# Moving the attention's early steps against the feed-forward chunks, in the batches after the first two

## The reference

```python
h = jnp.einsum('bhid,oi,od->bho', x, weighted_sum, weight)      # 'mix': 256 x 4 inputs -> 256 per token

t = layernorm(h)                                                # attention
q, k, v = split(t @ qkv_w.T + qkv_b)                            # 16 heads of 16
q, k = rotate(q), rotate(k)
q, k = q / norm(q), k / norm(k)
h = h + softmax(q @ k.T * HD ** -0.5) @ v @ out_w.T + out_b

t = layernorm(h)                                                # 8 experts, hidden width 1024
p = sigmoid(t @ Wg + bg)
w = p * (p > 0.5)
h = h + sum_e w[:, e] * (relu(t @ W1[e] + b1[e]) @ W2[e] + b2[e])
```

## Time and profile before

| | |
|---|---|
| median of 3 runs | 1918.91 us (1918.88 to 1920.49) |
| the profiled execution's own time | 1918.81 us |
| its span, first to last instruction | 1917.0 us |
| PE busy | 1838.3 us (96%) |
| ACT busy | 1077.8 us (56%) |
| DVE busy | 698.6 us (36%) |
| POOL busy | 628.7 us (33%) |

### The profile page before, as it was taken

The page is one execution under the profiler, slowest core; times in us unless marked ns, Lnnn a source line. Parts: engine busy times, 40 slices in busy tenths (PEclk is TensorE's granted clock), DMA queues, the critical chain, the costliest instruction groups (busy, mean ns, idle before and its releaser), DMA issues.

```text
span 1917.0 us, 31838 instructions
## 1 busy us (share of the span) xinstructions
PE 1838.3 (96%) x12652; PEld 1168.6 (61%) x12652; DVE 698.6 (36%) x1575; ACT 1077.8 (56%) x1658; POOL 628.7 (33%) x537
## 2 busy tenths in 40 slices
PE   5679899999999999999999999999999999999999
PEld 4156545775467754677547764577546775466666
DVE  7867644554023621346103460144401453022001
ACT  3744676546655476545765457644665546654444
POOL 1012323334233342333323242333423334234443
PEclk9789999999999999999999999999999999999999
DMA  4322433415123151223313341232512315213221
GB/s 163 112 108 89 132 126 139 176 56 132 67 90 120 67 132 67 103 96 100 110 45 111 121 111 67 77 127 73 132 67 88 121 67 131 69 67 103 107 98 46
DMA packets 103971, 192.31 MB, mean 100 GB/s; under 512 B 67448, under 2 KB 80656, under 8 KB 87440
## 3 DMA queue, kind: packets, MB, share of 16 engines
q1 hardware_dynamic: 103824, 190.28, 30.7%
HBM read 153.55 MB, written 20.97 MB: 91 GB/s over the span
## 4 chain that ended last, share of the span: by engine, by line
PE 85%; DVE 3%; DMA 2%; ACT 2%; issue 2%; SPq 0%; DVEq 0%; ACTq 0%
PE bank_h L995 32%; PE bank_f L1014 11%; PE bank_f L1017 10%; PE bank_f L1016 10%; PE bank_o L903 6%; PE bank_s L889 4%; PE bank_s L801 3%; PE bank_s L802 3%; PE bank_s L803 3%; DMA kt<-stack 1%; DMA kt<-probs 1%; ACT hh L778 1%; PE bank_m L915 1%; PE bank_s L949 1%; PE bank_m L810 1%
## 5 line engine op out<-in xcount | busy, mean ns | idle before, releaser
L644 POOL TENSOR_TENSOR hl<-h,hh 128x512 f16<-128x512 f32 x512 | 602.9, 1178 | 1202.7 <-ACT hh L778 688.4
L995 PE MATMUL bank_h<-x,w1s 128*128 128x512 f16 x3072 | 750.0, 381 | 5.2 <-ACT hh L778 4.6
L775 ACT ACTIVATE h<-bank_h,b1s 128x512 f32<-128x512 f32 x512 | 351.3, 686 | 479.4 <-PE bank_h L995 479.2
L1014 PE MATMUL bank_f<-w2s,hh 128*128 128x256 f16 x2048 | 560.4, 274 | 2.3 <-DVE acc L1255 2.3
L1017 PE MATMUL bank_f<-w2s,hl 128*128 128x256 f16 x2048 | 558.8, 273 | 0.0
L1016 PE MATMUL bank_f<-w2s,hh 128*128 128x256 f16 x2048 | 558.8, 273 | 0.0
L995 PEld LDWEIGHTS bank_h<-x,w1s 128*128 128x128 f16 x3072 | 287.9, 99 | 331.0 <-issue 43.7
L778 ACT ACTIVATE hh<-bank_h,b1s 128x512 f16<-128x512 f32 x512 | 349.9, 683 | 0.0
L744 ACT ACTIVATE probs<-bank_s 128x1024 f32<-128x1024 f32 x240 | 246.3, 1026 | 161.5 <-PE bank_s L889 160.6
L1014 PEld LDWEIGHTS bank_f<-w2s,hh 128*128 128x128 f16 x2048 | 201.4, 98 | 107.1 <-issue 40.6
L1255 DVE SCALAR_TENSOR_TENSOR acc<-bank_f,gw,acc 128x256 f32<-128x256 f32 x256 | 106.1, 477 | 368.9 <-PE bank_f L1017 368.7
(11 more groups left out here) (187 smaller groups left out, 1451.5 us busy)
## 6 DMA issues: line engine op xcount, KB each, us to landing
w1s<-w_parts SPq DMA_DIRECT2D x56, 1024.0 KB, 4.8
w2s<-w_parts SPq DMA_DIRECT2D x56, 1024.0 KB, 4.8
raw<-in_w_dram SPq DMA_DIRECT2D x16, 1024.0 KB, 6.6
xraw<-in_x_t_dram SPq DMA_DIRECT2D x30, 512.0 KB, 4.8
w_parts<-w1s SPq DMA_DIRECT2D x8, 1024.0 KB, 8.7
w_parts<-w2s SPq DMA_DIRECT2D x8, 1024.0 KB, 10.9
out_dram<-acc SPq DMA_DIRECT2D x16, 256.0 KB, 6.1
w1s<-in_x_t_dram SPq DMA_DIRECT2D x2, 512.0 KB, 8.6
```

The lines of the kernel that those rows point to most:

```text
L644: pool.tensor_tensor(hl[n % HBUFS][:], h32[n % 2][:], hh[n % HBUFS][:], ALU.subtract)\
L775: act.activation(h32[n % 2][:], bank_h[n % 2][:, :], ACT.Relu, bias=b1s[:, e, m:m + 1]).then_inc(h_hi.sem, 1)
L995: last = pe.matmul(bank_h[n % 2][:, :], w[:, wp, k, m * P:(m + 1) * P], x16s[fb % 2][:, xp, k, :], start=(k == 0 and wp + xp == 0), stop=( ...
L1014: pe.matmul(o, high, w[:, 0, m, :], start=(m == 0 and t % 2 == 0), stop=False, skip_group_check=True)
```

## The change

The due times of the steady list (`later` in the code: neither alone nor the first feed-forward) get their own tables. The other two lists come out as they were. In chunks, before and after:

| step | before | after |
|---|---|---|
| `mix` 0 to 3 | 2.1, 3.5, 4.9, 6.3 | 1.6, 2.7, 3.8, 4.9 |
| `ln1_turn` 0 to 3 | 9.0 + 1.5 t | 7.4 + 1.3 t |
| `qk_norm` | 15.7 | 13.2 |
| `stack` 0 to 3 | 18.85, 19.7, 20.5, 21.3 | 15.0, 15.85, 16.65, 17.45 |
| `out_bias` | 24.0 | 20.0 |
| `scores n` | 25.6 + 0.66 n | 20.2 + 0.80 n |

`weigh`, `out_copy`, `out_turn` and the attention's tail are tied to the pace and the first score, so the tail stays within a fraction of a chunk of where it was. In SP's queue `turn_stacks` moves ahead of expert 3's load.

```diff
-    mix, sooner, att_at = (FIRST_MIX, 1.5, FIRST_ATT) if first_ffn else (MIX, 0.0, range(TT))
+    later = not alone and not first_ffn
+    sooner, att_at = (1.5, FIRST_ATT) if first_ffn else (0.0, range(TT))
+    mix, unit = (FIRST_MIX, [u - 0.6 * sooner for u in UNIT]) if first_ffn else (LATER_MIX, LATER_UNIT)
+    turn, gap, norm = (LATER_TURN, LATER_GAP, LATER_NORM) if later else (9.0 - sooner, 1.5, 15.7 - sooner)
...
+    steps += [(mix[TT - 1] + 0.5, "ln1", 0), (norm, "qk_norm", 0), (20.0 if later else 24.0, "out_bias", 0)]
...
-    first = 25.6
+    first, pace = (LATER_FIRST, LATER_PACE) if later else (25.6, PACE)
     for n in range(2 * UNITS):
-        steps.append((first + PACE * n, "scores", n))
+        steps.append((first + pace * n, "scores", n))
...
-MIX = [2.1, 3.5, 4.9, 6.3]
+LATER_MIX = [1.6, 2.7, 3.8, 4.9]
+LATER_TURN, LATER_GAP, LATER_NORM = 7.4, 1.3, 13.2
+LATER_UNIT = [14.7, 15.55, 16.35, 17.15]
+LATER_FIRST, LATER_PACE = 20.2, 0.8
...
                 for e in range(2, EXPERTS):
-                    load_expert(b, e)
                     if more and e == 3:
                         turn_stacks(b + 1, range(TT))
+                    load_expert(b, e)
```

More of the change, by code:

```diff
@@ L62, in attention_order @@
     steps = []
-    mix, sooner, att_at = (FIRST_MIX, 1.5, FIRST_ATT) if first_ffn else (MIX, 0.0, range(TT))
+    later = not alone and not first_ffn
+    sooner, att_at = (1.5, FIRST_ATT) if first_ffn else (0.0, range(TT))
+    mix, unit = (FIRST_MIX, [u - 0.6 * sooner for u in UNIT]) if first_ffn else (LATER_MIX, LATER_UNIT)
+    turn, gap, norm = (LATER_TURN, LATER_GAP, LATER_NORM) if later else (9.0 - sooner, 1.5, 15.7 - sooner)
     for t in range(TT):
[L65 to L70, removed]
+        steps += [(mix[t - 1] - 0.05 if t else 0.3, "split", t), (mix[t], "mix", t), (turn + gap * t, "ln1_turn", t),
+                  (turn + 0.05 + gap * (t + 1), "qkv", t), (turn + 0.1 + gap * (t + 1), "rotate", t),
+                  (unit[max(t - 1, 0)] + 0.1 * min(t, 1), "unit", t), (unit[t] + 0.3, "stack", t)]
+    steps += [(mix[TT - 1] + 0.5, "ln1", 0), (norm, "qk_norm", 0), (20.0 if later else 24.0, "out_bias", 0)]
     if alone:
@@ L80, in attention_order @@
         steps.append((30.0, "out_bias", 0))
-    first = 25.6
+    first, pace = (LATER_FIRST, LATER_PACE) if later else (25.6, PACE)
     for n in range(2 * UNITS):
-        steps.append((first + PACE * n, "scores", n))
+        steps.append((first + pace * n, "scores", n))
     for u in range(UNITS):
-        steps.append((first + PACE * min(2 * u + 3, 2 * UNITS) + 1e-6, "weigh", u))
+        steps.append((first + pace * min(2 * u + 3, 2 * UNITS) + 1e-6, "weigh", u))
     for g in range(GROUPS):
-        steps += [(first + PACE * (8 * (g + 1) + 1) + 0.15, "out_copy", g),
-                  (first + PACE * (8 * (g + 1) + 3) + 0.2, "out_turn", g)]
-    tail = first + PACE * (2 * UNITS + 4) + 1
+        steps += [(first + pace * (8 * (g + 1) + 1) + 0.15, "out_copy", g),
+                  (first + pace * (8 * (g + 1) + 3) + 0.2, "out_turn", g)]
+    tail = first + pace * (2 * UNITS + 4) + 1
     for t in range(TT):
```

## The result

The changed kernel takes 1965.5 us, the median of 4 runs (1964.3 to 1967.4), against 1918.95 us before: a ratio of 1.0241, 95% interval 1.0225 to 1.0257. The forecast was 1962, 2.3% slower. The profiled execution took 1964.28 us, its span is 1962.5 us, 45.5 us longer than before.

What follows compares the result with a forecast made beforehand. PE bounds the kernel with 96% of the span, hardly waiting. Lost cover at the scores (6.0 us) and first mix (1.3 us) over six bodies adds 43.8 us to 1918.8: 1962 us, range 1945 to 1984.

Steps and rivals of the forecast that it cites:

- The chain of the scores: Last projection to `scores 0`: 26.4 us through norms, stacks and transpositions against 19.5 us of PE work; net +6.0 us a body.
- The first mix: PE reaches `mix 0` after two `f1` instead of three and waits for the split `xl`: +1.3 us a body.
- The sum: Six steady bodies, (6.0 + 1.3) x 6 = 43.8 us added to 1918.8: about 1962 us, 2.3% slower.
- the forecast's own range: Low (4.7 + 1.1) x 6 = 35 us, 1954; high (7.1 + 2.1 + 0.5) x 6 = 58 us, 1977.
- The pieces don't add to the 6.9: they lie inside it: PE's 6.9 us wait splits: about 1.3 us before `f1 19`, 2.5 before `f2 16`, about 3 at `scores 0`.
- three signs of being wrong: No PE idle before the scores, transpositions much under 14 us, or PEclk of 0.50 inside the steady bodies.
- The clock: Rival: new PE waits before the scores lower the clock, losing 4.7 us a body: 1990 us, or about 1976; chance 0.12.
- PEclk 1.00 throughout: Expected sign in the new profile: PE's clock stays full in each of the six steady bodies.
- the third piece: The rest of PE's 6.9 us wait, about 3 us a body, standing at `scores 0`.
- Edits at nothing: Later mixes, turns, `acc` of expert 0, expert 3's load and spread scores cost nothing; `acc` up to 0.5 us a body.
- Not slower, by a faster turning: Rival: without a load ahead, the eight transpositions take 8.8 us instead of 15.7: 1921 us, or 1914; chance 0.06.

Runs made afterwards that it cites:

- run with the mix back: The changed kernel with all four mixes half a chunk later (due 2.1, 3.2, 4.3, 5.4): 1956.35 us, 1.0194 of the kernel before.
- run with late scores: The changed kernel with only the scores back at their old due times (25.6 + 0.66 n): 1960.1 us, 1.0209 of the kernel before.
- run with the spread stacks: The changed kernel with the stacks of tiles 2 and 3 two to three chunks later, scores still at 20.2: 1980.9 us, 1.032 of the kernel before.
- run with the turning moved alone: The kernel before with the turning put ahead of expert 3's load and nothing else changed: 1981.4 us, 1.0326 of the kernel before.
- run with the load put first: The changed kernel with expert 3's load put back ahead of the turning in SP's queue: 2015.97 us, 1.0503 of the kernel before.

## Why the prediction was right, and where it was not

**The chain of the scores: right.** 26.7 us against 26.4, with small errors that cancel. `unit 0` started 7.9 us after the last projection where I had 8.4, but the two units took 2.27 us together where I had carried over 1.32, so the first transposition came 0.45 us late; the issues took 11.8 us instead of the mean of 12.4.

**The first mix: right.** +1.3 us a body forecast. In the third body the `f1` behind the mix starts 7.64 us after the first (848.79 to 856.43), where three `f1` and the mix before it needed the same 7.65 (831.60 to 839.25): the third `f1`, which I counted at 1.3 us, is now missing ahead of it. PE's wait there grew by 9.2 us in six bodies, 1.5 us each, and the run with the mix back gave 9.2 us for the 7.8 of the sum.

**The sum: right.** 43.8 us forecast; the medians differ by 46.6, the spans by 45.5. One bound of my range was added up wrong: with 13.25 and 3.9 us the wait is 10.6 + 13.25 + 3.9 + 0.1 - 19.5 = 8.35 us and not 7.9, so the high end of the forecast's own range was about 1979 us and not 1977.

**The step that failed: "The pieces don't add to the 6.9: they lie inside it", with "about 3 us" at `scores 0`.** The sizes of the first two were near (1.3 and 2.5 us forecast; 12.8 / 6 and 12.7 / 6, 2.1 each, measured), but the scores waited 1.0 / 6 = 0.2 us. "No idle of PE before the scores" and a PEclk of 0.50 inside the steady bodies were two of my three signs of being wrong. Both came, the first all but (1.0 us in six bodies), and yet the time came out. As an account of the sum the sentence held: `scores 0` started within 0.2 us of the landing in four bodies, whatever PE had waited for before. As an account of the causes it failed. I read the pieces as shares of one wait, that of the scores for the turning. They are a wait of their own as well: the run with late scores keeps them nearly whole. Two gates hang on the same transpositions. One is the stacks, through ACT's queue and DVE's; the other is the scores. That they are of nearly the same height here is chance: it let the one that I had computed give the right total. The words would have misled whoever went on to mend it: they say that later scores give back 6.0 us a body, and that gave 5.4 us in all.

**The clock: I gave it 0.12, and it fell in every steady body.** "PEclk 1.00 throughout" was wrong. Over the six bodies of the change 30.7 us ran at 0.50, against none before. PE had work in 26.5 us of them, so about 13.2 us were lost, 2.2 us a body. My time did not suffer, since nearly all of it lay ahead of the scores, where PE would have waited: it took the place of the third piece. I had judged by the length of one idle that had cost nothing, and that reading was luck. The same idle stands in the trace of the change, 2.31 us in front of the same `f2` in the start phase, and there 3.4 us at 0.50 follow it:

```profile
207.70:211.50 3.80, 3.80 (x16) 2.20 (x17) 3.80 (x6) 2.93 (x5) 1.80 (x2) 0.55 0.96 195
```

Nor did it take two pieces each time. In four of the steady bodies the clock fell behind the second idle, but in the third body at 921.5, before the second began, and in the second body in the midst of a first one of 3.7 us.
The Trainium skill (TensorE: Matmul & The Clock Gate, HAM oscillation — how this bites in real kernels) tells of a kernel that waits for a DMA between short bursts of matmuls and goes back to the half clock at each of these waits. The run with the spread stacks agrees, in six of six waits of 6.2 to 7.7 us for the transpositions; of the shorter waits at the first mix, 1.9 us each, none of six brought the clock down in the change, and three of six did in that run.

**Edits at nothing.** The later mixes and `acc` of expert 0: no wait names them. Spreading the scores: nothing was to be won, since they wait 1.0 us in all. Expert 3's load: right for the change, where no wait names `w1s`, but the reason that I gave, three chunks of cover behind `scores 0`, is not the one that matters: the run with late scores has no such cover and no such wait. The room comes from the stacks, and so the turning, being early. The run with the turning moved alone cost 62 us for the lack of it.

**Not slower, by a faster turning: false.** First to last issue is still 11.8 us with no load ahead (11.3 to 13.1 us over the six bodies).
The Trainium skill (DMA: Bandwidth & Descriptors, Issuing engines are not separate DMA queues) says that all DMAs run on the same 16 engines and interleave. The run with the load put first agrees in that a transposition right behind a load took over 6 us instead of 3.3, and the eight of them 14.6 us; but in the kernel before the load left 3.2 us ahead of them (899.19 against 902.43), and there taking it away changed little: 12.3 us with it and 11.9 without, on the mean of six bodies.

## What to carry to other kernels

When work is moved earlier and something waits, list every instruction that hangs on the slow step, each on its own engine's queue: undoing one part can show almost nothing, or make it worse, while another gate of the same height stands, and only the two together tell the price. What an order of instructions places between the two ends of a wait is the cover of that wait; ask of each moved transfer what stood between it and its reader, since a move that costs nothing in one order cost 62 us in the other. And an idle of PE can cost more than its length, by the clock behind it: the waits of 6.2 to 7.7 us here did each time, those of about 2 us sometimes, so one short idle that left the clock alone is no proof for the next.

## What the runs showed of the hardware

- The length of a short idle of PE did not tell whether the granted clock fell to half. The same idle of 2.31 us left it at 1.00 in the trace of before and had 3.4 us at 0.50 behind it in the trace of the change; the idles of 1.9 us at the first mix had such a stretch behind them in none of six bodies of the change and in three of six with the stacks spread.
- 58 matmuls that nobody needs, put into a wait of some 7 us, six times, made the kernel with that wait 6.9 us faster (1980.9 to 1974.0 us).
- A transposition issued 0.4 us behind the second half of a load on the same queue released its reader 6.6 us later; the third body of before shows 3.1 to 3.9 us from issue to landing for `kt`, and in the change the reader follows 3.35 us behind the issue (913.09 to 916.44).
